# Macaron block on one core: the routed rows gathered by an inverted slot table, and the experts' outputs combined by accumulating transfers

## The reference, cut to what matters

```python
x = x + 0.5 * ffn(layernorm(x))     # x: 4096 tokens x 256, f32
x = x + attention(layernorm(x))
x = x + 0.5 * ffn(layernorm(x))     # the same weights again

def ffn(x):                         # 8 experts, two per token, cap = 1228 rows each
    logits = x @ router_w + router_b
    top_k_logits, expert_indices = top_k(logits, 2)
    probs = softmax(top_k_logits)
    pos = place of the pick in its expert (all first picks, then all second)
    einp[expert, pos] += x          # a pick with pos >= cap is dropped here ...
    h = einp @ w_c_fc + b_c_fc;  g = einp @ w_gate + b_gate      # 256 -> 1024
    o = silu(h * g) @ w_c_proj + b_c_proj                        # 1024 -> 256
    return sum over k of probs[k] * o[expert_k, pos_k]           # ... but reads row cap - 1 here

def attention(x):                   # 16 heads of 64 x 64, a gated linear recurrence
    q, k, v = x @ W_q, x @ W_k, x @ W_v;  a = sigmoid(x @ W_gate + b_gate)
    S = a * S + k v^T;  o = q S     # over the tokens
    return o @ W_o
```

## Time and profile before

| | us |
|---|---|
| three timed runs, median | 2362.4 |
| lowest and highest of them | 2360.11, 2366.91 |
| the profiled execution, its own time | 2361.27 |
| its span in the trace | 2359.5 |
| PE busy in the span | 2005.5 (85%) |
| DVE, ACT, POOL busy | 1415.8, 1019.3, 263.9 |
| the whole chain that ended last: PE, DVE, issue, POOL | 69%, 12%, 11%, 3% |

### The profile page before, as it was taken

How to read it: one execution, slowest core, us unless ns; L and a number is a source line. 1 busy time by engine, 2 the same in 40 slices (tenths; PEclk the granted TensorE clock), 3 DMA queues, 4 the chain that set the end, 5 groups by cost and what they waited for, 6 DMA issues and landing times.

```text
span 2359.5 us, 37052 instructions
## 1 busy us (share of the span) xinstructions
PE 2005.5 (85%) x13127; PEld 1706.8 (72%) x13128; DVE 1415.8 (60%) x3224; ACT 1019.3 (43%) x1798; POOL 263.9 (11%) x267
## 2 busy tenths in 40 slices
PE   5159999999995999999999999870799999999860
PEld 5148888888884877877778777770688888888660
DVE  6335665566555758668686695653455555666452
ACT  1045666656463433334333333210555665666420
POOL 1620000000002100101001000027000000000524
PEclk9999999999997999999999999955899999999985
DMA  6242221222122000000000000014222222222204
GB/s 261 89 160 81 98 81 62 72 98 98 41 86 66 19 5 13 18 0 18 9 9 18 0 0 1 1 36 148 86 81 63 80 72 80 88 75 83 81 31 138
DMA packets 95354, 150.12 MB, mean 64 GB/s; under 512 B 9583, under 2 KB 76678, under 8 KB 94068
## 3 DMA queue, kind: packets, MB, share of 16 engines
q1 hardware_dynamic: 83008, 116.46, 14.5%
q0 software_dynamic: 12288, 32.91, 4.4%
HBM read 98.84 MB, written 51.15 MB: 64 GB/s over the span
## 4 chain that ended last, share of the span: by engine, by line
PE 69%; DVE 12%; issue 11%; POOL 3%; ACT 1%; another core or an unknown queue 1%; SPq 1%; DMA 1%; DVEq 0%; POOLq 0%
PE bank L574 32%; PE bank L324 13%; PE bank L326 7%; PE bank L641 5%; PE bank L665 4%; DVE wide L1329 2%; POOL halves L469 2%; PE bank L555 2%; PE bank L710 1%; PE bank L714 1%; DVE wide L1331 1%; DVE wide L1301 1%; DVE halves L1357 1%; DVE wide L1315 1%; PE bank L682 1%
## 5 line engine op out<-in xcount | busy, mean ns | idle before, releaser
L574 PE MATMUL bank<-halves 128*128 128x512 f32 (+2 forms) x3744 | 767.3, 365 | 22.5 <-issue 18.1
L574 PEld LDWEIGHTS bank<-halves 128*128 128x128 f32 x3744 | 645.3, 190 | 130.5 <-issue 27.1
L324 PE MATMUL bank<-halves 128*128 128x512 f32 (+1 forms) x1352 | 480.7, 399 | 15.7 <-DVE halves L1357 11.4
L326 PE MATMUL bank<-halves 128*128 128x256 f32 (+1 forms) x1352 | 379.0, 280 | 0.0
L828 ACT ACTIVATE temp<-bank,bias_now 128x512 f32<-128x512 f32 (+1 forms) x312 | 200.3, 642 | 360.9 <-PE bank L574 345.3
L1164 DVE SCALAR_TENSOR_TENSOR temp<-bank,bias_fc,temp 128x512 f32<-128x512 f32 (+1 forms) x312 | 216.0, 692 | 219.7 <-ACT temp L828 214.9
L324 PEld LDWEIGHTS bank<-halves 128*128 128x128 f32 (+1 forms) x1352 | 252.1, 186 | 81.7 <-DVE halves L1357 13.5
L641 PE MATMUL bank<-halves 128*128 128x512 f32 x1152 | 286.3, 400 | 2.0 <-issue 2.0
L1171 DVE TENSOR_TENSOR halves<-temp,halves 128x512 fp32r<-128x512 f32 (+1 forms) x312 | 198.0, 635 | 126.4 <-ACT halves L781 121.8
L326 PEld LDWEIGHTS bank<-halves 128*128 128x128 f32 (+1 forms) x1352 | 253.5, 188 | 0.4
L641 PEld LDWEIGHTS bank<-halves 128*128 128x128 f32 x1152 | 212.0, 189 | 50.0 <-issue 2.4
(11 more groups left out here) (157 smaller groups left out, 2114.9 us busy)
## 6 DMA issues: line engine op xcount, KB each, us to landing
expert_out<-rows SPq DMA_DIRECT2D x144, 128.0 KB, 1.7
wide<-in_L_ffn_w_c_fc SPq DMA_DIRECT2D x16, 1024.0 KB
wide<-in_L_ffn_w_gate SPq DMA_DIRECT2D x16, 1024.0 KB
wide<-in_L_ffn_w_c_proj SPq DMA_DIRECT2D x16, 1024.0 KB
wide<-expert_in SPq DMA_DIRECT2D x32, 512.0 KB, 4.8
expert_in<-halves SPq DMA_DIRECT2D x9, 1024.0 KB
x<-in_L_attn_x SPq DMA_DIRECT2D x4, 1024.0 KB, 9.5
out_x<-x SPq DMA_DIRECT2D x32, 128.0 KB
```

What stands on the lines that cost most here:

```text
L324: nc.tensor.matmul(out_, a[0][:, k, of], v[:, k].rearrange("p a n -> p (a n)"), start=(k == 0), stop=False, skip_group_check=True)
L326: ins = nc.tensor.matmul(out_[:, 0:C], a[1][:, k, of], v[:, k, 0, :], start=False, stop=(k == last), skip_group_check=True)
L574: m = pe.matmul(bank[at + b][:, 0:w], a[:, kc, j * P:(j + 1) * P], v[:, kc, 0:w], start=(i == 0), stop=(i == len(ps) - 1))
```

## The change

- **The slot table is inverted on chip.** DVE compares each pick's slot, split into its column (one of COLS = 80: 10 tiles of 128 slots for each of 8 experts) and its rank in the tile, with all columns and all ranks (`match`, two instructions for each of six chunks: four quarters of 8 tiles of picks, then two chunks of 16). ACT multiplies the column matches by the token's partition (`by_partition`), POOL by the pick's number (`by_pick`), and PE sums 64 matmuls 128x160 of rank by column (`invert`). From the bank DVE makes x_index (the token of each slot), y_index (the same, out of range for an empty slot) and weight_index.
- **Gathers instead of scatters.** SP stores xn to xn_rows in DRAM (four DMAs of 1 MB per FFN). POOL gathers the rows of each tile of slots straight into PE's input (`gather_rows`, 10 DMAs per expert), and the combine's weight of each slot (`gather_weights`, 10 DMAs of one element per partition). expert_in, its clears and the loads from it are gone.
- **Accumulating transfers instead of the combine.** SP writes x_in to sum_rows in DRAM (4 MB). ACT multiplies a summed y tile by its slots' weights (`weigh`) into a ring of four, and POOL adds it with an indirect DMA that accumulates (`add_rows`, 10 per expert) into sum_rows for the first FFN, into `out` for the second. The adds of tiles 0 and 1 wait until all adds of the expert before have landed. expert_out, its stores, the gathers from it, DVE's `combine`, `combine_last` and the last 32 stores are gone. SP loads x from sum_rows ahead of the attention (8 loads of 512 KB, one after the other) and stores it to `out` in the attention (8 stores).
- **Order.** The group of 204 rows comes first (now group 0, tiles 0 and 1), then the two of 512. ACT weighs tiles 0 and 1 within the units of the last group, and the other eight behind its copies of the next expert's weights, where it waits for each y sum. DVE's y_out waits for the weighing two tiles back, no longer for a store. Both turns of the next expert stand within the down products. The `If` around the 204 rows is now one of three places with a switch of ACT's function table per expert, where there were two.
- **Dropped picks.** DVE makes a table of dropped weights (`drop`). SP stores each expert's last slot row (`store_last`) and, in the last expert, loads them with 16 small DMAs (`load_table`). PE turns the weights (`turn_dropped`) and adds the dropped rows in 16 jobs of two matmuls of K = 32, N = 256 (`add_dropped`), in the last expert alone: two behind each unit from the third on of its last group, and two each behind y tiles 2 and 3. Job n waits for the copy of job n - 2. ACT copies the even jobs, DVE the odd ones, and POOL adds each to DRAM by a plain accumulating DMA of 256 KB.

**Constants.** The order of a row group and the sizes of the table:

```diff
-GROUPS = [(s, min(512, CAP - s)) for s in range(0, CAP, 512)]
...
+GROUPS = [(1024, CAP - 1024), (0, 512), (512, 512)]
...
+Y_TILES = len(SLOT_TILES)
+FIRST = [sum(len(t) for t in GROUP_TILES[:n]) for n in range(3)]
+COLS = E * Y_TILES
+RING = 4
+JOBS = 16
...
+JOB_TILES = [16 * (n // 8) + 4 * (2 * (n // 4 % 2) + n % 2) + 2 * (n // 2 % 2) for n in range(JOBS)]
```

```diff
-            def load_rows(r, e, n):
...
+            def store_xn(r, q):
+                sp.wait_ge(xn_made, r * TILES + (q + 1) * QT)
+                sp.dma_start(xn_rows[q * QT * P:(q + 1) * QT * P, :].rearrange(tok, p=P),
+                             xn[:, q * QT:(q + 1) * QT, :]).then_inc(xn_stored, 16)
...
-            def store_y(r, e, t):
+            def store_last(r, e):
                 u = r * E + e
-                sp.wait_ge(y_copied, u * Y_TILES + t + 1)
...
+                sp.wait_ge(y_summed, u * Y_TILES + 2)
+                sp.dma_start(last_rows[bass.ds(e, 1), :], y_sb[CAP - 1 - 1024 - P:CAP - 1024 - P, 1, :]).then_inc(last_stored, 16)
...
+            def load_table(r):
...
+                for n in range(SUPER):
+                    for m in range(SUPER):
+                        at = 32 * n + E * m
+                        sp.dma_start(last_table[at:at + E, m, :], last_rows[:, :]).then_inc(table_loaded, 16)
...
+                if r == 0:
+                    sp.dma_start(sum_rows[:, :], x_in[0]).then_inc(rows_begun, 16)
+                sp.wait_ge(weights_made, r + 1)
+                sp.dma_start(weight_rows.rearrange("(p j) a -> p (j a)", p=P), weights[:]).then_inc(weights_stored, 16)
...
+                all_added(r)
...
+                    for s in range(NSUP):
+                        i = s * SUPER
+                        sp.dma_start(x[:, i:i + SUPER, :],
+                                     sum_rows[i * P:(i + SUPER) * P, :].rearrange(tok, p=P)).then_inc(x_back, 16)
+                        sp.wait_ge(x_back, (s + 1) * 16)
```

```diff
+            def by_pick(r, n):
+                picks = chunk(n)
+                pool.wait_ge(matched, r * CHUNKS + n + 1)
+                nc.gpsimd.tensor_tensor(by_column[:, picks, COLS:2 * COLS], matches[n],
+                                        pick_ranks[:, picks].unsqueeze(2).to_broadcast([P, picks.stop - picks.start, COLS]),
+                                        ALU.mult).then_inc(by_pick_made, 1)
...
+            def gather_rows(r, e, n):
...
+                for i in range(len(GROUP_TILES[n])):
+                    col = e * Y_TILES + GROUPS[n][0] // P + i
+                    pool.indirect_dma_start(xg[buf][:, i, :], None, xn_rows,
+                                            bass.IndirectOffsetOnAxis(ap=x_index[:, col:col + 1], axis=0)
+                                            ).then_inc(xg_loaded[buf], 16)
...
+            def gather_weights(r, e):
...
+                    pool.indirect_dma_start(slot_weight[:, col:col + 1], None, weight_rows,
+                                            bass.IndirectOffsetOnAxis(ap=weight_index[:, col:col + 1], axis=0)
+                                            ).then_inc(weight_got, 16)
...
+            def add_rows(r, e, tiles):
...
+                for t in tiles:
...
+                    pool.wait_ge(y_weighted, u * Y_TILES + t + 1)
+                    pool.indirect_dma_start((sum_rows, out[0])[r],
+                                            bass.IndirectOffsetOnAxis(ap=y_index[0:m, col:col + 1], axis=0),
+                                            weighted[0:m, t % RING, :], None, bounds_check=T - 1, oob_is_err=False,
+                                            compute_op=ALU.add).then_inc(y_added[t % RING], 16)
...
+            def add_jobs(r):
...
+                for n in range(JOBS):
+                    i = JOB_TILES[n]
+                    pool.wait_ge(job_copied[n % 2], r * JOBS // 2 + n // 2 + 1)
+                    pool.dma_start((sum_rows, out[0])[r][i * P:(i + 2) * P, :].rearrange(tok, p=P),
+                                   staged[:, n % 8, :].rearrange("p (a c) -> p a c", c=C),
+                                   accum_op=ALU.add).then_inc(job_added[n % 8], 16)
...
-                        pool.indirect_dma_start(expert_in,
-                                                bass.IndirectOffsetOnAxis(ap=write_slot[:, j:j + 1], axis=0),
...
+                for n in range(CHUNKS):
+                    by_pick(r, n)
+                pool.wait_ge(x_index_made, r + 1)
...
+                gather_rows(r, 0, 0)
+                gather_rows(r, 0, 1)
...
+                for e in range(E):
+                    gather_rows(r, e, 2)
+                    if e == 0:
+                        pool.wait_ge(*((rows_begun, 16), (stored, NSUP * 16))[r])
+                    else:
+                        landed(r, e - 1, Y_TILES)
+                    add_rows(r, e, range(2))
+                    if e + 1 < E:
+                        pool.wait_ge(xg_turned, (r * E + e) * NG + 3)
+                        gather_rows(r, e + 1, 0)
+                        gather_rows(r, e + 1, 1)
+                        gather_weights(r, e + 1)
+                    else:
+                        landed(r, e, 2)
+                        add_jobs(r)
+                    add_rows(r, e, range(2, Y_TILES))
```

**PE.** TensorE:

```diff
+                def invert(r):
...
+                        for j in range(chunk(n).start, chunk(n).stop):
+                            m = pe.matmul(bank[0][:, 0:2 * COLS], by_low[n][:, j - chunk(n).start, :], by_column[:, j, :],
+                                          start=(j == 0), stop=(j == PICKS - 1))
+                    m.then_inc(inverted, 1)
...
+                    if last and n == 2 and j >= 2:
+                        add_dropped(r, 2 * (j - 2))
+                        add_dropped(r, 2 * (j - 2) + 1)
...
+            def add_dropped(r, n):
...
+                else:
+                    pe.wait_ge(job_copied[n % 2], r * JOBS // 2 + n // 2)
+                for k in range(2):
+                    m = pe.matmul(bank[6 + n % 2][:, k * C:(k + 1) * C], dropped_turned[at:at + 32, h, :],
+                                  last_table[at:at + 32, (i + k) % 4, :], start=True, stop=True)
+                m.then_inc(job_done, 1)
...
+                if last:
+                    add_dropped(r, 12)
+                    add_dropped(r, 13)
+                down(r, e, 1, range(1, 2))
+                if last:
...
+                else:
+                    turn(r, e + 1, 0)
+                down(r, e, 1, range(2, 4))
...
-                down(r, e, 1, range(2, 3))
...
-                    down(r, e, 1, range(3, 4))
+                    turn(r, e + 1, 1)
+                down(r, e, 2, range(3))
```

**ACT.** ScalarE:

```diff
+            def by_partition(r, n):
...
+                nc.scalar.activation(by_column[:, chunk(n), 0:COLS], matches[n], ACT.Copy,
+                                     scale=partition[:, 0:1]).then_inc(by_partition_made, 1)
...
+                def weigh(t):
...
+                    act.wait_ge(y_summed, u * Y_TILES + t + 1)
...
+                    act.wait_ge(y_added[t % RING], (u * uses_in_ring(t) + t // RING + 1) * 16)
+                    nc.scalar.activation(weighted[0:m, t % RING, :], y_sb[0:m, t % 2, :], ACT.Copy,
+                                         scale=slot_weight[0:m, bass.ds(e * Y_TILES + SLOT_TILES[t], 1)]
+                                         ).then_inc(y_weighted, 1)
...
+                        if 2 * HJ < unit < 2 * HJ + 3:
+                            weigh(unit - 2 * HJ - 1)
...
+                        if last and unit >= 2 * HJ + 2:
+                            copy_job(r, 2 * (unit - 2 * HJ - 2))
...
+                for t in range(2, Y_TILES):
+                    if not last and t in (4, 6):
+                        turned(r, e + 1, t // 2 - 2)
...
+                    weigh(t)
```

**DVE.** VectorE:

```diff
+                v.tensor_tensor(matches[n], tile_ranks[:].unsqueeze(1).to_broadcast([P, m, COLS]),
+                                column[:, picks].unsqueeze(2).to_broadcast([P, m, COLS]),
+                                ALU.is_equal).then_inc(matched, 1)
+                v.tensor_tensor(by_low[n], low_ranks[:].unsqueeze(1).to_broadcast([P, m, P]),
+                                low[:, picks].unsqueeze(2).to_broadcast([P, m, P]), ALU.is_equal).then_inc(low_matched, 1)
...
+                match(r, QUARTERS)
+                match(r, QUARTERS + 1)
...
+                dve.wait_ge(inverted, r + 1)
...
+                v.tensor_scalar(x_index, found, float(P), 0.0, ALU.subtract, ALU.max).then_inc(x_index_made, 1)
...
+            def drop(r):
...
+                v.tensor_tensor(dropped, dropped, dropped_part, ALU.add).then_inc(dropped_made, 1)
+                v.memset(last_table, 0.0).then_inc(table_cleared, 1)
...
                 def y_out(t):
...
-                    dve.wait_ge(y_stored[t % 2], (u * (Y_TILES // 2) + t // 2 + 1) * 16)
...
+                    wait_past(dve, y_weighted, u * Y_TILES + max(t - 1, 0))
+                    if t == 3:
```

(9 more changed lines are left out.)

502 lines of the change are left out of this document (286 added, 216 removed).

## The result

The changed kernel takes 2611.45 us (median of four runs, 2603.49 to 2616.05) against 2364.65: a ratio of 1.1041, 95% interval 1.1006 to 1.1076. It is 247 us slower, where 96 us faster was forecast; the range (2215 to 2315) did not hold it.

The account below looks back on a forecast made before the run. PE was taken to bound the experts and nearly the attention, leaving 218 us of gaps to win from. The terms, -26 - 33 + 27 + 15 + 7 - 7 - 9 - 70, gave -96: 2265 us, range 2215 to 2315.

Parts of the forecast that it names:

- Term D: The 14 looped experts: PE's work the same, adds and weighings fit into idle POOL and ACT; +7 us (-5 to +40).
- R4: Rival: more waits on nothing on the core, in longer code that runs once; three more of 8 us, 2290; chance 0.12.
- Term C: Last expert of each FFN: jobs of dropped picks stall on copies and the table; +27 us first, +15 second.
- credit of 12 us: Second FFN's last expert: gathers of the first rows vanish, and with them ACT's waits; 12 us less.
- A: First routing, to the experts' first product: 24.6 us in place of 52.6, +2 ahead; -26 us (-12 to -35).
- upper bound that I set from a select: First routing, by_pick of 1280 elements on POOL: 2.9 us from POOL's select of 0.29 for 128 columns.
- B: Second routing: the first routing's chain against 60.3 us, 24.6 + 2.5; -33 us (-20 to -42).
- G: The end, behind the last product: 76.7 us become 6.5; -70 us (-72 to -60).
- E: Start of the attention: 18.7 us ahead of the statistics become 11 to 12; -7 us (-12 to 0).
- F: Inside the attention: DVE loses 64 combine instructions, 30.5 us, and steps g shorten; -9 us (-15 to 0).
- R1: Rival: ring of four weighed tiles binds if an add's landing exceeds 9 us; at 25 us some 2520; chance 0.06.

Follow-up runs that it names:

- e8_weights_spread: The changed kernel with the next expert's 10 weight gathers one behind each add of tiles 2 to 9 and two at the end, everything computed: 2532.38 us.
- e2_before_gathers: The kernel before with 16 one-element gathers added on POOL in each of the 14 looped experts, read by nobody: 2528.44 us, ratio 1.0701.

## Why the prediction was wrong

**Term D failed**: "+0.5 each" for the 14 looped experts, from "POOL is idle half the time" and ten weighings of ScalarE "in its 38% of idle time". Engine shares were summed as if a DMA on POOL cost only POOL. The looped experts lost 20 us each. Without the weight gathers 12 of these go (169 of 279 us in all), and with the gathers spaced the same; the late sums of tiles 0 and 1 take 2 (28 us); 4.8 each, 67 in all, are left without all three, and 15 are not assigned. PE's clock is part of each of them: behind its wait from 273.84 to 284.24 the granted clock was 0.50, the level of 1.2 GHz, from 284.20 to 289.00, and the mean was 0.92 in the expert above. The trace of before had the sign of it: ScalarE's 10.00 and 8.06 us in the earlier trace rows stood in streams of POOL's scatters and gathers. I read them as something of code that runs once (R4, +25 us, 0.12) and took the gain of their going, without asking what a stream of 16 in each expert would do.

**Term C was mis-sized**: the jobs cost 86 us where 27 in each layer were taken, the last experts 84 where 42 were. The matmuls cost the 8 forecast and 5 more, 1.6 ns a column where the sum has 1, which no row of before shows; and behind them PE and ScalarE waited for each other in turn. The credit of 12 us in the second layer came as a difference: without jobs its last expert is 87.9 us (before 94.9), and the first layer's is 86.0 (before 80.8).

**A** gave 18.4 of 26: up to the last slots the routing was 3.6 us shorter (2 longer forecast), and the chain behind took 37.7 in place of 24.6. by_pick is 4.31 us where 2.9 was taken, so the upper bound that I set from a select was none; the second turn's rows came 5.9 us behind the last row gather (114.84), and PE then idled 6.08 us for nothing the profile shows, while POOL issued ten weight gathers, until 127.4:

```profile
91.20 1.49 DVE L1286 TENSOR_TENSOR x<-tile_ranks,temp 128x1280 bf16<-128x1280 bf16 x1
92.77 4.31 POOL L524 TENSOR_TENSOR x<-x,pick_ranks 128x1280 bf16<-128x1280 bf16 x1 [5.93 <-DVE x L1286]
94.81 3.61 DVE L1286 TENSOR_TENSOR temp<-tile_ranks,temp 128x1280 bf16<-128x1280 bf16 x1
120.78 1.97 PE L674 MATMUL bank<-ident,wide 128*128 128x128 f32 x8 [7.70 <-DMA wide<-xn_rows,x]
128.84 0.80 PE L692 MATMUL bank<-halves 128*128 128x512 f32 x1 [6.08 <-issue]
```

**B** has the right number (-32.8 for -33) by luck: from the last slots to the first product it took 31.3 us in place of 24.6, and the routing ahead of them was 4 us shorter, not longer. **G** was nearly right (-64.4 for -70; POOL's adds, 1.56 + 0.30 each, were still in line behind the last tile). **E** gave 2.2 of 7: at the last product four adds were still in line on POOL, the last of them until 901.3. **F** failed on a small scale: 30.5 us of VectorE went and the attention kept its length, 749.3 to 748.4. The trace after has steps of 8.42 us (1240.67 to 1249.09, by the rows of PE's transposes) beside others of 8.90 (1275.05 to 1283.95) without any combine, so the difference between the steps in the earlier trace rows was not the combine's. The trace of before says it outright: the step from 1115.28 to 1124.17 that the earlier trace rows takes for one with a combine has no row of line 1226, and a step that has one (1168.68 to 1177.05, the combine at 1171.79) took 8.37 us.

**R1** had its 2520 on the right side of the forecast for a reason that did not occur. Of the landing of an accumulating transfer the page shows the jobs' alone, beside plain ones:

```profile
sum_rows<-x POOLq DMA_DIRECT2D x16, 256.0 KB, 5.8
x<-sum_rows SPq DMA_DIRECT2D x8, 512.0 KB, 3.8
out_x<-x SPq DMA_DIRECT2D x8, 512.0 KB, 2.9
```

256 KB take 5.8 us where 512 KB without an add take 3.8 and 2.9. The Trainium skill, "Collectives: The Full Stack", section "Why ReduceScatter is half of AllGather", gives half the rate for an add in the DMA. The rows here point the same way, by a larger factor; they do not part the add from POOL's queue, so they do not show it.

## What to carry to other kernels

A run of POOL's indirect gathers, 16 in 20 us, made PE's signals reach ScalarE and VectorE some 10 us late, though nobody waited for what they moved. In the old kernel a wait for each landing took the whole loss away; in the new one pauses after every third gather, together with another place for the gathers, gave back 173 of 181 us. Before work is moved to an idle engine, look for waits without a releaser in the stretches where that engine is already busy, and try the instructions alone, with nobody reading them, in the old kernel. When a mend gives back less than it should, look again at who waits: the spread gathers of e8_weights_spread had cured the stall and made the queue late. And a copy that an in-order engine must make for another belongs ahead of the instruction that waits for that other's next work.

## What the runs showed of the hardware

- The stalls above: 16 indirect gathers in a row cost a looped expert 11.8 us, 8 up to 6, 4 none, 16 with pauses none, 32 plain DMAs of 0.54 us each none, gathers and adds in turn for 33 us none.
- In these stalls the wait is for PE's signal, whose step the trace has 9.8 us (e2_before_gathers) and 13.7 us (the changed kernel) behind the end of the product in the two timelines above.
- An indirect gather keeps POOL for 0.95 us (0.30 more until the next), an accumulating one for 1.56, a plain one for 0.54.
- A compare of 1280 bf16 elements on VectorE took 1.49 us alone and 3.61 when it began within POOL's product of 1280 (4.31 us), in the rows above; it ended 1.3 us behind that product.
